# The last two weight tiles of a head are split in its own first body instead of in the last body of the head before

## The reference, cut to what matters

```python
mixed = hidden_states @ W_qkv
mixed = _causal_conv_silu(mixed.transpose(0, 2, 1), conv_w).transpose(0, 2, 1)
...
z = (hidden_states @ W_z).reshape(Bb, Tt, HV, DV)
...
def step(S, inp):
    qt, kt, vt, gt, bt = inp
    S = S * jnp.exp(gt)[..., None, None]
    v_adj = (vt - jnp.einsum('bhk,bhkv->bhv', kt, S)) * bt[..., None]
    S = S + kt[..., None] * v_adj[..., None, :]
    o = jnp.einsum('bhk,bhkv->bhv', qt, S)
    return (S, o)
```

## Time and profile before

| | before |
|---|---|
| median of 3 runs (lowest to highest) | 2390.62 us (2385.49 to 2390.97) |
| the profiled execution, its own time | 2390.52 us |
| its span, first to last instruction | 2388.8 us |
| mean granted clock of TensorE | 0.954 |
| PE busy | 2084.1 us (87%) |
| DVE busy | 1808.6 us (76%) |
| ACT busy | 1585.6 us (66%) |
| POOL busy | 844.0 us (35%) |
| code brought by the queue q14 | 30 packets, 0.25 MB |

### The profile page before, as it was taken

One profiled execution on the slowest core, in us unless ns is written; L12 is line 12 of the kernel. 1 busy time (PEld: TensorE's weight loads), 2 busy tenths in 40 slices (PEclk: granted clock), 3 DMA queues, 4 the chain that ended last, 5 costly groups with the idle time before them and its releaser, 6 DMA issues. The chain is left out here.

```text
span 2388.8 us, 56369 instructions
## 1 busy us (share of the span) xinstructions
PE 2084.1 (87%) x19224; PEld 1527.4 (64%) x19224; DVE 1808.6 (76%) x4220; ACT 1585.6 (66%) x4442; POOL 844.0 (35%) x806
## 2 busy tenths in 40 slices
PE   5699999999999999999999999758988998757998
PEld 2477777777777777777777777645666666524444
DVE  8677777777777777777777777636888888764997
ACT  2677777777777777777777777536767767633343
POOL 7223222222222222222222232213566666550332
PEclk8799999999999999999999999779999999877999
DMA  2100000000000000000000000053333332113111
GB/s 73 50 9 22 31 9 25 28 9 24 28 9 26 26 9 26 26 9 26 26 9 26 26 9 26 14 180 87 98 93 99 97 88 88 44 42 121 56 55 51
DMA packets 122858, 107.57 MB, mean 45 GB/s; under 512 B 12080, under 2 KB 97072, under 8 KB 122800
## 3 DMA queue, kind: packets, MB, share of 16 engines
q1 hardware_dynamic: 122800, 106.87, 14.3%
HBM read 72.24 MB, written 34.60 MB: 45 GB/s over the span
## 5 line engine op out<-in xcount | busy, mean ns | idle before, releaser
L603 PE MATMUL proj<-xn_hi,w_lo 128*128 x768 | 361.0, 470 | 0.0
L604 PE MATMUL proj<-xn_lo,w_hi 128*128 x768 | 306.3, 399 | 0.0
L605 PE MATMUL proj<-xn_hi,w_hi 128*128 x768 | 305.4, 398 | 0.0
L974 DVE SCALAR_TENSOR_TENSOR qkv<-conv_in,taps,qkv 128x512 f32<-128x512 f32 x384 | 290.4, 770 | 9.0 <-ACT qkv L832 9.0
L1211 POOL TENSOR_TENSOR r_norm<-sumsq,neg_half 128x8 f32<-128x8 f32 x32 | 67.3, 2102 | 646.9 <-DVE sumsq L1137 646.9
L1192 POOL TENSOR_TENSOR o_pow<-o_var,neg_half 128x4 f32<-128x4 f32 x68 | 89.4, 1331 | 424.7 <-DVE o_var L1006 424.7
L1087 DVE TENSOR_TENSOR i_less_r<-bank_c,join_mask 128x256 f16<-128x256 f32 x330 | 124.9, 420 | 143.3 <-PE bank_c L668 143.3
L898 ACT ACTIVATE inv<-bank_b 128x256 f16<-128x256 f32 x330 | 109.2, 381 | 134.7 <-PE bank_b L688 134.6
L605 PEld LDWEIGHTS proj<-xn_hi,w_hi 128*128 128x128 f32 x768 | 145.8, 190 | 34.8
L603 PEld LDWEIGHTS proj<-xn_hi,w_lo 128*128 128x128 f32 x768 | 145.6, 190 | 25.8
L851 ACT ACTIVATE g_mask<-mask_ge,g_cols 128x128 fp32r<-128x128 f32 x528 | 157.8, 399 | 0.0
(11 more groups left out here) (290 smaller groups left out, 5989.6 us busy)
## 6 DMA issues: line engine op xcount, KB each, us to landing
out_t<-o_out SPq DMA_DIRECT2D x68, 256.0 KB, 2.0
o_raw<-out_t SPq DMA_DIRECT2D x32, 512.0 KB, 5.4
w_raw<-in_L_attn_W_qkv_dram SPq DMA_DIRECT2D x36, 256.0 KB, 2.8
wq_dram<-wq_q SPq DMA_DIRECT2D x48, 128.0 KB, 1.8
w_raw<-in_L_attn_W_z_dram SPq DMA_DIRECT2D x18, 256.0 KB, 2.7
x_sb<-in_x_dram SPq DMA_DIRECT2D x16, 256.0 KB, 2.8
x_in<-in_x_dram SPq DMA_DIRECT2D x16, 256.0 KB, 5.8
wq_raw<-in_L_ffn_w_gate_dram SPq DMA_DIRECT2D x16, 256.0 KB, 2.6
```

Of the source, the lines that this page charges most:

```text
L603: pe.matmul(out, w_lo[:, k, cols], sh.xn_hi[:, k, tok], start=(k == 0), stop=False)
L604: pe.matmul(out, w_hi[:, k, cols], sh.xn_lo[:, k, tok], start=False, stop=False)
L605: product = pe.matmul(out, w_hi[:, k, cols], sh.xn_hi[:, k, tok], start=False, stop=(k == KT - 1))
L974: dve.scalar_tensor_tensor(out=out, in0=conv_in[:, j, :, k:k + T], scalar=taps[:, j, k:k + 1], in1=out, op0=ALU.mult, op1=ALU.add).then_in ...
```

## The change

ScalarE and VectorE split only tiles 0 to 3 of the next head in the last body of a head. Tiles 4 and 5 are split in the first body of the head that they belong to: by ScalarE in levels 1 and 2, by VectorE in levels 2 and 3 (`this_g`). So that the first body can have them, it gets a copy of its own: the inner loop now runs over passes 1 and 2 alone. Ahead of the loop only tiles 0 to 3 of the first head are split. TensorE, GpSimd and SyncE keep their code. In the built program the loop over heads is now 391 instructions long on VectorE and some 399 on ScalarE.

```diff
+        LATE = 4
...
-                def step(n, project, next_g):
+                def step(n, project, this_g, next_g):
...
+                            if this_g is not None and l in (1, 2):
+                                split(this_g, 3 + l)
                             if next_g is not None and l in (0, 1, 5):
                                 split(next_g, l if l < 2 else 2)
...
-                    if next_g is not None:
-                        for j in (4, 5):
-                            split(next_g, j)
-
-                for j in range(TILES):
+                for j in range(LATE):
                     split(0, j)
                 mask_gates(0, None)
                 with act.Fori(0, HK) as g:
-                    with act.Fori(0, PAIRS - 1) as p:
-                        step(PAIRS * g + p, True, None)
-                    step(PAIRS * g + PAIRS - 1, True, g + 1)
-                step(STEPS, False, None)
+                    step(PAIRS * g, True, g, None)
+                    with act.Fori(1, PAIRS - 1) as p:
+                        step(PAIRS * g + p, True, None, None)
+                    step(PAIRS * g + PAIRS - 1, True, None, g + 1)
+                step(STEPS, False, None, None)
...
+                            if this_g is not None and l in (2, 3):
+                                split(2 + l, TILES * this_g + 3 + l)
                             if next_g is not None and l in (1, 3):
                                 split(l // 2, TILES * next_g + l // 2 + 1)
...
-                    if next_g is not None:
-                        for j in (4, 5):
-                            split(j, TILES * next_g + j + 1)
-
-                for j in range(TILES):
+                for j in range(LATE):
                     split(j, j + 1)
...
-                    with dve.Fori(0, PAIRS - 1) as p:
-                        step(PAIRS * g + p, True, None)
-                    step(PAIRS * g + PAIRS - 1, True, g + 1)
-                step(STEPS, False, None)
+                    step(PAIRS * g, True, g, None)
+                    with dve.Fori(1, PAIRS - 1) as p:
+                        step(PAIRS * g + p, True, None, None)
+                    step(PAIRS * g + PAIRS - 1, True, None, g + 1)
+                step(STEPS, False, None, None)
```

## The result

The changed kernel takes **2401.4 us** (median of 6 runs, 2399.4 to 2403.6) against 2390.8 for the kernel before on the same chip: a ratio of 1.0047, 95% interval 1.0036 to 1.0058. The profiled span is 2399.0 us, 10.2 more than before. So the kernel is slower, by less than forecast, and the terms of the sum can be read one by one. Lines of the changed kernel are numbered a little differently: the transposes of L652 are L653 there, and the `taps` copies L1173 and L1174.

A forecast was written before the change was run, and what follows sets the result against it. VectorE's order was taken to set the time at head borders, with TensorE's clock falling behind the longer idle stretch. From 2390.5 us, +12.25 at borders, +4.2 for the clock and -2.85 at prologue and end gave 2404 us, range 2395 to 2420.

The forecast's parts named there:

- Part 4: Loop over heads, three body copies on ScalarE and VectorE: a fifth code block doesn't fit, 2.8 us wait per border.
- The stall: Wait for code at the branch back to the loop's head, at every border, both engines: 2.8 us, chance 0.81.
- The bounds: Limits for the wait at each border: 2.0 us, quickest landing of any transfer, to 5.0 us, landing of the smallest.
- Part 1: At the seven borders between heads: the splits leave, which gives back 1.05 us per border.
- The clock: TensorE's clock falls in all seven first bodies behind a border, 2.0 us each: 14.0 against 9.8, +4.2 us.
- Part 2: In a head's first body: the splits moved into its levels are hidden and cost nothing.
- The sign named for it: In first bodies, TensorE's way from L652 to L664 stays at 18.09 us; if longer, Part 2 is wrong.
- Part 3: Before the loop and after the last head: 1.8 us and another 1.05 us saved, together -2.85 us.
- The sum: Whole kernel: +12.25 us at seven borders, +4.2 for the clock, -2.85 at prologue and end: +13.6, 2404 us.
- the code stays in: Rival for the borders: no wait for code, each border 1.05 us shorter, clock stays up; 2370.5 us, chance 0.12.

The follow-up runs named there:

- e1: The changed kernel with the loop over heads written out on both ScalarE and VectorE, so no branch back: 2374.0 us.
- e3: The changed kernel with the loop over heads written out on ScalarE alone: 2401.6 us.
- e5: The kernel before with only the third copy of the body added on ScalarE and VectorE, no split moved: 2409.55 us.
- e10: The kernel before with 42 one-column writes ahead of VectorE's loop over heads, meant to make it touch four code blocks: 2435.0 us.
- e2: The changed kernel with the loop over heads written out on VectorE alone: 2375.9 us.
- e6: The kernel before with 53 one-column writes ahead of VectorE's loop over heads, to shift its code addresses: 2407.0 us.
- e9: e8 with one of VectorE's splits in the last body moved behind the tap that follows it: 2368.6 us.
- e4: The kernel before with the loop over heads written out on both ScalarE and VectorE: 2398.1 us.
- e8: e1 with the loads of the next head's tiles 1 and 2 put behind the stores of the first two bodies: 2374.3 us.
- e7: The kernel before with 70 one-column writes ahead of VectorE's loop over heads: 2392.5 us.

## Why the prediction was right, step by step

**Part 4, the code, carried it and held.** The stall was put at 2.8 us; VectorE stands 2.56, and the way from `o` to `taps` fits: 0.67 without a wait (e1), 3.32 with it, 2.65 more. The bounds, 2.0 and 5.0 us, held as well: the waits behind the branch take 2.2 to 3.2 us over all borders of after, e3, e5 and e10. (The bounds were medians of groups of transfers, and not the quickest and slowest single one.) That four blocks are the store was my choice from rows that bore out only "four and no more"; e10 shows it. The Trainium skill ("Runtime: NRT & Kernel Launch", Instruction fetch mechanics) gives most engines 32 KiB, and four blocks of 8 KB agree. It has refills of 16 KiB; q14's blocks here are 8 KB, also in e10. Two details were wrong. I expected two blocks per engine and border; it is all five (102 packets, not 60), which fits a store that drops what is wanted next. That cost nothing more: the trace shows no such wait in mid-body. And the stall is on both engines, but e2 and e3 show that VectorE's alone makes the loss: ScalarE's 1.25 us lie beside it.

**Part 1, what the border gives back, held.** 1.05 us was taken. Without the 2.56 of standing the way from `o` to `taps` would be 0.76 instead of 1.88, so 1.12. That makes 2.56 - 1.12 = 1.44 net per border, and the transposes do come 1.43 later behind the scores (10.67 us on average, 9.24 before); forecast was 1.75. Of the difference, 0.24 are the stall's size and 0.07 what was given back. Where the loop is written out (e1), `taps` to `g_cols` is 0.3 shorter as well, so first bodies there take 43.6 and not the 44.1 that the rival gave.

**The clock** fell at all seven, as forecast, for 1.88 us each on average against 2.0. (From the transposes to a body's end it is 35.92 us in the one such body before in which the clock stayed up, so 251.4 for seven; after, the seven take 264.6.) The reason given was too simple. It said that the clock "fell in none of 24 bodies" behind 1.38 us of idle, and let the length of the stretch decide. In e6 it fell in second bodies behind 1.44 to 1.48, in e9 in a third one behind 1.42; in e2 it stayed up in four first bodies behind 1.61 to 1.66 and fell in the three others behind 1.60 to 1.76; it stayed up in e4 three times behind 2.93 to 2.97. The length of one idle stretch does not decide it. What does is open.

**Part 2, the splits at nothing, held.** The sign named for it came: in e1, where nothing covers an extra cost, TensorE goes from the transposes to L665 in 18.1 us in first bodies, and these, with two splits on each engine, are as long as ordinary ones without.

**Part 3, prologue and end: both gains came, and one was lost again.** The first `g_mask` starts at 75.81 (forecast 75.8), the first body 1.82 us earlier (forecast 1.8); the end gave 1.10 (forecast 1.05). But the first body itself takes 46.17 instead of 44.38. This is the sentence that failed: SyncE's loads wait for the later splits, and only "the store of the first body is queued behind". The cost of the later transfers was put at nothing. But the loads themselves now start at 103 us and the stores at 107, and TensorE stands for 1.57 us for its code. In e8, with the loads moved on, the pause is 0.20 and the body 44.61.

**The sum.** Forecast +12.25 at the borders, +4.2 for the clock, -2.85: +13.6. Measured in the loop: first bodies +13.4 instead of 16.45, made of 7 x 1.43 = 10.0 at the borders instead of 12.25 and 3.4 for the clock instead of 4.2 (13.1 for seven falls, against 9.8 before and 14.0 forecast); start -1.8; first head's first body +1.8; other bodies -1.2, since ordinary second ones take 43.53 instead of 43.65. That makes +12.15. The end takes off 1.10, and the stages behind the loop, which the change doesn't touch, another 0.85: +10.2. That the number came so near is partly luck: the borders and the clock were 3.05 us too dear, and 1.8 of it was cancelled by the first body's loss, which was not foreseen. The 1.2 of the other bodies and the 0.85 behind the loop were not in the sum either.

**The rival** "the code stays in" gave 2370.5 for a world without the stall. e1 is that world: 2374.0. The rival took off the clock's whole loss of 9.8; in e1 some 6 of it came back in four middle bodies, and the first body took 1.4 more than before, 1.03 of it TensorE's pause. Against that, each border is 0.5 shorter than the rival had it, 3.5 for seven.

## What to carry to other kernels

A copy of a loop's body is not free even where it adds no work: count the code blocks that the loop touches, at both ends, and the one fetched ahead. A third copy here cost 17.6 us in a change that otherwise wins. Written out without an outer loop, the same order is 18 us faster than the kernel before, since the code of VectorE and ScalarE, met only once, came ahead of its use. Which address the loop happens to lie at is worth 44 us in e10, so an edit ahead of such a loop can cost more than the edit is worth. When you move a split, follow the loads that wait for it: they, too, get a new time, and what is under way then can suffer. And read the rows before believing a total: e6 was slower by another cause than the one it was built for.

## What the runs showed of the hardware

- VectorE with 269 instructions in a loop keeps them if they touch three blocks of 8 KB (before, e6, e7: 30 or 31 packets), and fetches all anew at each pass if they touch four (e10: 65). An exposed wait of VectorE took 2.2 to 3.2 us behind the branch (2.50 to 2.74 after, 2.23 to 2.51 in e5, 2.90 to 3.23 in e10), and a second one of 1.4 to 1.7 followed in e10.
- TensorE stood for 1.57 us where a block of its code (q8, 16 KB) was fetched while transfers held 26% of the DMA engines, for 1.03 in e1, and for 0.20 when they were moved away (e8). In later heads q8 brings nothing, and there is no such pause.
- TensorE's clock fell behind idle stretches of 1.42 us and stayed up behind some of 2.97. From run to run the falls moved to other bodies, at 1.2 to 2.5 us each; in e4, which missed its forecast by 7 to 10 us, the five falls outside the first bodies make some 7.
